# A gated sparsifier over 32 images: the end of the period reordered on TensorE, ScalarE, VectorE and GpSimd

## The reference

```
v = group_norm(x, 32 groups of 16 channels)
r = relu(v)
r = 0 in channels where max(r) - mean(r) < 0.5
bb = 1 - exp(-|max over channels of r - mean over channels of r|)    per pixel
y = bb * r
control1 = sigmoid(mean_pixels(y) @ W1.T)
control3 = relu(mean_pixels(y) @ W3.T), 1.2 where below 1
thres = control1 * control3 * max_pixels(y)                            per channel
out = x + (y where y >= thres, else 0)
```

## Time and profile before

| | |
|---|---|
| median of 3 runs | 1692.47 us (1690.44 to 1693.3) |
| the profiled execution | 1694.59 us, span 1692.8 us |
| VectorE busy | 1459.9 us, 86% |
| ScalarE busy | 1355.9 us, 80% |
| TensorE busy | 1266.6 us, 75% |
| GpSimd busy | 610.5 us, 36% |
| mean granted TensorE clock | 0.868 of full |
| DMA queues | 61.1% and 30.1% of 16 engines' span |

### The profile page before, as it was taken

One profiled execution on the slowest core, in us unless ns is written; L12 is line 12 of the kernel. 1 busy time (PEld: TensorE's weight loads), 2 busy tenths in 40 slices (PEclk: granted clock), 3 DMA queues, 4 the chain that ended last, 5 costly groups with the idle time before them and its releaser, 6 DMA issues.

```text
span 1692.8 us, 26138 instructions
## 1 busy us (share of the span) xinstructions
PE 1266.6 (75%) x9888; PEld 883.0 (52%) x9888; DVE 1459.9 (86%) x2192; ACT 1355.9 (80%) x2177; POOL 610.5 (36%) x446
## 2 busy tenths in 40 slices
PE   3788777887777888777788877778877778877761
PEld 1555455555555555455555555555545555555550
DVE  2588889988889898888998888998888989888896
ACT  6788888788888788888878888888888888888821
POOL 0032334442344442244443243443233444224440
PEclk8988888998788998888898888899888899888885
DMA  9259999999999999999999999999999999999973
GB/s 394 112 127 318 340 355 311 291 314 303 338 350 324 287 316 301 339 343 341 299 303 307 316 343 346 299 309 313 311 342 351 318 299 316 292 340 342 302 228 152
DMA packets 93345, 517.64 MB, mean 306 GB/s; under 512 B 10272, under 2 KB 10272, under 8 KB 93216
## 3 DMA queue, kind: packets, MB, share of 16 engines
q1 hardware_dynamic: 75360, 416.38, 61.1%
q0 software_dynamic: 17856, 99.56, 30.1%
HBM read 310.38 MB, written 205.52 MB: 305 GB/s over the span
## 4 chain that ended last, share of the span: by engine, by line
PE 40%; POOL 28%; ACT 20%; DVE 7%; issue 3%; DMA 1%; DVEq 0%; SPq 0%; ACTq 0%
POOL xs L788 25%; PE ps_gate L331 11%; PE ps_gate L298 10%; PE ps_turn L288 8%; ACT rs L482 6%; ACT rs L457 6%; ACT xs L482 4%; PE ps_gate L318 3%; PE ps_gate L360 2%; PE ps_gate L368 2%; POOL rstd L767 2%; PE ps_gate L306 2%; DVE xs L649 2%; ACT junk L433 1%; DVE max_and_mean L632 1%
## 5 line engine op out<-in xcount | busy, mean ns | idle before, releaser
L632 DVE TENSOR_REDUCE max_and_mean<-ps_turn 128x2 f32<-128x1024 f32 x384 | 463.6, 1218 | 31.8 <-PE ps_turn L288 28.1
L288 PE MATMUL ps_turn<-ident,xs 128*128 128x128 f32 (+1 forms) x1600 | 359.6, 311 | 175.2 <-DVE max_and_mean L632 112.0
L788 POOL TENSOR_TENSOR xs<-xs,rs 128x1568 f32<-128x1568 f32 x124 | 433.3, 3531 | 1.8 <-DVE rs L680 1.8
L779 POOL DMA_DIRECT2D xs<-in_x x124 | 111.5, 968 | 889.4 <-DVE xs L680 796.9
L433 ACT ACTIVATE junk<-xs 128x1568 bf16<-128x1568 f32 x256 | 385.4, 1505 | 9.8 <-ACT junk L433 0.4
L318 PE MATMUL ps_gate<-ident,bb 128*128 128x128 f32 (+1 forms) x1600 | 272.2, 332 | 156.3 <-ACT bb L475 150.8
L288 PE MATMUL ps_turn<-ident,rs 128*128 128x128 f32 (+1 forms) x1600 | 345.7, 302 | 0.0
L318 PEld LDWEIGHTS ps_gate<-ident,bb 128*128 128x128 f32 (+1 forms) x1600 | 248.8, 239 | 175.9 <-DVE ymax_parts L649 163.7
L288 PEld LDWEIGHTS ps_turn<-ident,xs 128*128 128x128 f32 (+1 forms) x1600 | 209.0, 155 | 248.2 <-DVE max_and_mean L632 158.4
L649 DVE CUSTOM_DVE_ANT_0 xs<-xs,ps_gate 128x768 f32<-128x768 f32 (+1 forms) x256 | 243.1, 958 | 48.7 <-PE ps_gate L318 48.5
L457 ACT ACTIVATE xs<-xs,shift,rstd 128x3136 f32<-128x3136 f32 x64 | 192.0, 3001 | 86.0 <-POOL shift L771 80.8
(11 more groups left out here) (80 smaller groups left out, 955.7 us busy)
## 6 DMA issues: line engine op xcount, KB each, us to landing
xs<-in_x SPq DMA_DIRECT2D x260, 784.0 KB, 13.7
out<-xs SPq DMA_DIRECT2D x256, 784.0 KB, 8.2
xs<-in_x POOLq DMA_DIRECT2D x124, 784.0 KB, 10.9
rs<-in_L_conv_W SPq DMA_DIRECT2D x2, 1024.0 KB, 17.5
```

The costliest lines, as they stand in the source:

```text
L288: mm = pe.transpose(ps_turn[0:w, n % 2, b - 2 * i, P * t:P * (t + 1)], r_tile(s, t)[:, P * b:P * b + w], ident[:, :])
L632: ins = dve.tensor_reduce(max_and_mean[:, 2 * i:2 * i + 2, 0], ps_turn[:, n % 2, :, :], AX.X, ALU.max)
L779: pool.dma_start(half(x_tile(s - 1, t), h), dram_half(x_tiles, s - 1, t, h), accum_op=ALU.add).then_inc(x_added[(s - 1) % XR][t][h], 16)
L788: pool.tensor_tensor(o, o, half(r_tile(s - 1, t), h), ALU.add).then_inc(added, 1)
```

## The change

On TensorE all sums of x of the next image come right behind the logits, then the mean rows of the first three tiles in number order, the group statistics, the mean rows of the last tile, a turn, the turning of the means, a turn, and the first spread. ScalarE squares whole tiles (only the first tile stays in halves) into an 8-bit scratch, takes row means and group copy ahead of the copied mean rows, and does the first relu ahead of copying the means; the gate values of group 3 stand ahead of the last relu, three pooling sums ahead of these. VectorE does the first differ behind blocks 3 and 4, the peaks and fails behind all gates of group 2, and the settling right behind the count. GpSimd's affine stands ahead of the fourth accumulating DMA and is one instruction shorter (the row mean comes negated).

```diff
-        junk = sb("junk", [P, HALF], BF16)
+        junk = sb("junk", [P, HW], FP8)
@@ TensorE, per period
-                mean_rows_of(s)
                 if s + 1 < B:
-                    sum_x(s + 1, range(0, 2))
-                turn_means(s)
-                if s + 1 < B:
-                    sum_x(s + 1, range(2, T))
-                turn(s, 3)
-                turn(s, 4)
+                    sum_x(s + 1, range(T))
+                mean_rows_of(s, range(0, T - 1))
                 if s + 1 < B:
                     group_stats(s + 1)
+                mean_rows_of(s, range(T - 1, T))
+                turn(s, 3)
+                turn_means(s)
+                turn(s, 4)
                 spread(s, 0)
@@ TensorE, group statistics
-                pe.wait_ge(squared, 2 * T * (s + 1))
-                for h in range(2):
-                    mm = pe.matmul(ps_group[:, 1, :], group_avg[:, :], squares[:, h, :], start=(h == 0),
-                                   stop=(h == 1), skip_group_check=True)
-                mm.then_inc(group_sums, 1)
+                pe.wait_ge(squared, (T + 1) * (s + 1))
+                first = LOAD_ORDER[0]
+                pe.matmul(ps_group[:, 1, :], group_avg[:, :], squares[:, 0:T], start=True, stop=False,
+                          skip_group_check=True)
+                pe.matmul(ps_group[:, 1, first:first + 1], group_avg[:, :], squares[:, T:T + 1],
+                          start=False, stop=True, skip_group_check=True).then_inc(group_sums, 1)
@@ ScalarE, squares and row means
+            def square_tile(s, n):
                 t = LOAD_ORDER[n]
-                act.wait_ge(x_loaded[s % XR][t][h], 16 * (s // XR + 1))
+                wait_loaded(act, s, t)
+                square(s, t, slice(0, HW), t)
...
-                                          scale=1.0 / (PER_GROUP * HW), accum_out=row_sum[:, :]))
+                                          scale=-1.0 / (PER_GROUP * HW), accum_out=row_sum[:, :],
+                                          saturate=False))
@@ ScalarE, per period
                     square_tile(s + 1, 1)
-                copy_mean_rows(s)
-                if has_next:
                     square_tile(s + 1, 2)
-                copy_means(s)
                 if has_next:
                     square_tile(s + 1, 3)
                     row_means(s + 1)
+                    copy_group(s + 1)
+                copy_mean_rows(s)
+                if has_next:
+                    relu(s + 1, RELU_ORDER[0])
+                copy_means(s)
                 gate_values(s, 0)
-                if has_next:
-                    copy_group(s + 1)
-                    relu(s + 1, RELU_ORDER[0])
                 gate_values(s, 1)
                 if has_next:
                     relu(s + 1, RELU_ORDER[1])
                     relu(s + 1, RELU_ORDER[2])
                 gate_values(s, 2)
-                pool_sum(s, 0, 0)
+                for t in range(3):
+                    pool_sum(s, 0, t)
+                gate_values(s, 3)
                 if has_next:
                     relu(s + 1, RELU_ORDER[3])
-                gate_values(s, 3)
-                for t in range(1, T):
-                    pool_sum(s, 0, t)
+                pool_sum(s, 0, 3)
@@ VectorE, per period
+                if s > 0:
+                    keep_tile(s - 1, KEEP_ORDER[3])
+                block_max(s, 3)
+                block_max(s, 4)
                 differ(s, 0)
-                if s > 0:
-                    keep_tile(s - 1, KEEP_ORDER[3])
-                for i in range(3, 6):
-                    block_max(s, i)
+                block_max(s, 5)
                 differ(s, 1)
...
-                gate(s, 2, 0)
-                gate(s, 2, 1)
-                gate(s, 2, 2)
+                for t in range(T):
+                    gate(s, 2, t)
                 if nxt < B:
                     peaks(nxt)
-                gate(s, 2, 3)
-                if nxt < B:
                     margins(nxt)
                     find_fails(nxt)
                 gate(s, 3, 0)
                 if nxt < B:
                     read_count(nxt)
-                gate(s, 3, 1)
-                if nxt < B:
                     settle_channels(nxt)
-                gate(s, 3, 2)
-                gate(s, 3, 3)
+                for t in range(1, T):
+                    gate(s, 3, t)
@@ GpSimd
-                steps.step(pool.tensor_tensor(mrs[:, :], gst[:, 0, :], rstd[:, :], ALU.mult))
-                steps.wait()
-                pool.tensor_scalar(shift[:, :], mrs[:, :], -1.0, 1.0, ALU.mult, ALU.mult).then_inc(affine_ready, 1)
+                pool.tensor_tensor(shift[:, :], gst[:, 0, :], rstd[:, :], ALU.mult).then_inc(affine_ready, 1)
...
+                    accumulate(s - 1, 0, 0)
+                    accumulate(s - 1, 0, 1)
+                    accumulate(s - 1, 1, 0)
                 if s + 1 < B:
                     affine(s + 1)
+                if s > 0:
+                    accumulate(s - 1, 1, 1)
```

More of the change, by code:

```diff
@@ L6 @@
 F32 = mybir.dt.float32
-BF16 = mybir.dt.bfloat16
+FP8 = mybir.dt.float8e4
 I32 = mybir.dt.int32
@@ L98, in gated_sparsifier @@
         half_neg = sb("half_neg", [P, T])
-        squares = sb("squares", [P, 2, T])
+        squares = sb("squares", [P, T + 1])
         row_sum = sb("row_sum", [P, 1])
@@ L106, in gated_sparsifier @@
         rstd = sb("rstd", [P, T])
-        mrs = sb("mrs", [P, T])
         shift = sb("shift", [P, T])
@@ L290, in turn, with mean_rows_of @@
                 mm.then_inc(t_filled, 1)
-            def mean_rows_of(s):
+            def mean_rows_of(s, tiles):
                 if s > 0:
                     pe.wait_ge(gated, T * (NG * s - 1))
-                for n in range(T * NM):
+                for n in range(NM * tiles.start, NM * tiles.stop):
                     t, j, k = n // NM, n % NM, n % 4
@@ L300, in mean_rows_of @@
                                    stop=(n >= T * NM - 4), skip_group_check=True, tile_position=(0, 32 * k))
-                mm.then_inc(mean_rows_mm, 1)
+                if tiles.stop == T:
+                    mm.then_inc(mean_rows_mm, 1)
             def turn_means(s):
@@ L427, in _, with square, square_half @@
             junk_step = Steps(act, squared)
-            def square_half(s, n, h):
-                t = LOAD_ORDER[n]
-                act.wait_ge(x_loaded[s % XR][t][h], 16 * (s // XR + 1))
[L432 to L438, removed]
+            def square(s, t, cols, part):
+                junk_step.wait()
+                junk_step.step(act.activation(junk[:, cols], x_tile(s, t)[:, cols], ACT.Square,
+                                              scale=float(HW) ** -0.5, accum_out=squares[:, part:part + 1],
+                                              saturate=False))
+            def square_half(s, h):
+                t = LOAD_ORDER[0]
+                act.wait_ge(x_loaded[s % XR][t][h], 16 * (s // XR + 1))
+                square(s, t, slice(HALF * h, HALF * (h + 1)), t if h == 0 else T)
+            def square_tile(s, n):
+                t = LOAD_ORDER[n]
+                wait_loaded(act, s, t)
+                square(s, t, slice(0, HW), t)
             def row_means(s):
@@ L492, in _ @@
             act.wait_ge(consts_ready, 1)
-            for n in range(T):
+            for h in range(2):
+                square_half(0, h)
+            for n in range(1, T):
                 square_tile(0, n)
@@ L503, in _ @@
                 if has_next:
-                    square_half(s + 1, 0, 0)
+                    square_half(s + 1, 0)
                 if s > 0:
@@ L507, in _ @@
                 if has_next:
-                    square_half(s + 1, 0, 1)
+                    square_half(s + 1, 1)
                 if s > 0:
@@ L697, in _ @@
                         keep_tile(s - 1, t)
-                differ(s, 0)
                 if s > 0:
                     keep_tile(s - 1, KEEP_ORDER[3])
-                for i in range(3, 6):
-                    block_max(s, i)
+                block_max(s, 3)
+                block_max(s, 4)
+                differ(s, 0)
+                block_max(s, 5)
                 differ(s, 1)
@@ L768, in affine, with accumulate @@
                 steps.wait()
-                steps.step(pool.tensor_tensor(mrs[:, :], gst[:, 0, :], rstd[:, :], ALU.mult))
-                steps.wait()
-                pool.tensor_scalar(shift[:, :], mrs[:, :], -1.0, 1.0, ALU.mult, ALU.mult).then_inc(affine_ready, 1)
+                pool.tensor_tensor(shift[:, :], gst[:, 0, :], rstd[:, :], ALU.mult).then_inc(affine_ready, 1)
+            def accumulate(s, t, h):
+                pool.wait_ge(kept, T * s + KEEP_ORDER.index(t) + 1)
+                pool.dma_start(half(x_tile(s, t), h), dram_half(x_tiles, s, t, h),
+                               accum_op=ALU.add).then_inc(x_added[s % XR][t][h], 16)
             affine(0)
@@ L775, in _ @@
                 if s > 0:
-                    for t in IN_PLACE:
```

(9 more changed lines are left out.)

## The result

The changed kernel takes 1933.27 us (median of 4 runs, 1929.63 to 1934.3), the kernel before 1692.39 (4 runs, 1690.44 to 1693.3). The ratio is 1.142 with a 95% interval of 1.140 to 1.144: slower by 241 us, 7.8 in each of 31 periods.

A forecast was written before the change was run, and what follows sets the result against it. VectorE with the small chain behind it was taken as the bound. 8.7 - 0.1 = 8.6 us in 30 periods (258), plus 3.5 and 2.5 for first and last, on 1694.59 gave 1958.6, stated as 1955; range 1815 to 1980.

The forecast's parts named there:

- held, clock down: GpSimd's affine held by VectorE's thresholding, spread 0 and turn 5 at half clock: 8.6 us a period, 1955 us; chance 0.55.
- the first rival: GpSimd's affine not held by the thresholding: 1818 us with clock up, 1875 with it down, centre 1835; chance 0.27.
- Affine held to the end of the thresholding: GpSimd's affine, ready at 866.97, waits out VectorE's thresholding of tile 3: full hold of 2.8 us, affine 869.75 to 871.95.
- the relu I had put for them: ScalarE's whole-tile squares priced like a relu of the same size: 3.01 + 0.18 us each.
- The sequel behind the late differ is bare: Gate values, spread and turn 5 no longer hidden under VectorE work; block 5 begins at 878.95, plus 6.8 us.
- my 8.7 us for the start of block 5: VectorE's block 5 begins at 880.85 instead of 872.13: 6.8 us, plus 1.9 for the half clock.
- The clock: TensorE's 5.6 us idle brings half clock to spread and turn 5: 1.4 to 2.3 us more, taken as 1.9.
- held, but the clock stays up: Affine held, TensorE not slowed: net 6.7 us a period, 1902 us; lower end of the forecast's own range, no separate chance.
- End of the period: Last group's gates, peaks, count and settling: gain 1.05 us, bare settling 0.95 us, net minus 0.1 a period.
- a gain of 1.05: VectorE from group 3's differ to its first gate: 5.0 us instead of 6.1, through earlier gate values and less idle.
- the settling follows the copy at once and its 0.95 us are bare: VectorE's settling, today under a 0.94 us gate, lies bare behind the copy of the flag: 0.95 us lost.
- Faster: VectorE loses both waits, logits and last group's gates (140 us), and pays 104: 1658 us; chance 0.05.

The follow-up runs named there:

- x3: Changed kernel with the thresholding of the last tile replaced by a one-operand maximum over it (all images but the last): 1829.9 us, ratio 1.081.
- the probe: Kernel before with a 128x4 memset and a 128x4 product added on GpSimd while VectorE thresholds tile 1: 1690.71 us in one run.
- y1: Kernel before with only the first differ moved behind the last thresholding and blocks 3 and 4 on VectorE: 1828.3 us, ratio 1.081.
- x6: Changed kernel with 22 unused identity products on TensorE between the turn of block 4 and the first spread: 1932.62 us, ratio 1.142.
- x4: Changed kernel with the settling of channels put back behind the second gate of group 3: 1929.23 us, ratio 1.140.
- y3: Kernel before with only the end of the period in the changed kernel's order, the settling left in place: 1650.15 us, ratio 0.975.
- x2: Changed kernel with copying the means and the gate values of group 0 ahead of relu of tile 0 on ScalarE: 1863.55 us, ratio 1.101.

## Why the prediction held, step by step

Forecast 1955, measured 1933. The forecast's own case (held, clock down) is the one that came. The range of 1815 to 1980 would have held the first rival too, so it is the profile and x3, not the time, that tell them apart.

- *Affine held to the end of the thresholding.* Shown by the timeline (989.73 against 989.67), the probe and x3. The first rival, no hold, was priced at 1835; x3, which takes the hold away, came to 1829.9. The group sums were ready 3.2 us ahead of the thresholding's end, 2.8 by the working: the whole-tile squares (2.82 + 0.19 us) were cheaper than the relu I had put for them. Under the hold this was worth nothing. The ground on which I took the full hold was weaker than it looked: the idle of the fourth accumulating DMA ends 0.6 to 1.8 us behind the third thresholding, in the midst of the fourth, while a held computation ends 0.06 us behind the operation that holds it. That the two are the same hold is not shown; that the hold came out as full as this row suggested was in part luck.
- *The sequel behind the late differ is bare.* Shown by y1, 4.4 us a period alone. Of my 8.7 us for the start of block 5, VectorE's waits show 7.9. Measured from the end of the thresholding: differ 5.4 us (5.8 by the working: GpSimd's steps and the relu 0.4 less), spread 0 begins 1.1 behind the differ (0.9), block 5 begins 3.9 behind the spread (4.45); that is the period shown, and the idles before block 5 vary by 0.7 over the inner periods.
- *The clock.* At its place it is 1.7 us a period (x6), 1.9 by the working. As a term of the whole it is not what I took it for: x6 got it back and ended no faster, since the end of the period lost the same. The sum held because the kernel pays for the half clock at one place or another. That the clock would have to stay up at the end of the period too for the rival "held, but the clock stays up", 1902, is what x6 suggests; no run had it up at both.
- *End of the period.* I had a gain of 1.05 and a loss of 0.95. The failed step is "the settling follows the copy at once and its 0.95 us are bare": bare it is (35.8 us over 31 periods, 1.15 each), but x4 shows that covering it is worth 0.1 us a period on balance. And I counted the gain from the missing idle alone, 1.05; by itself (y3) it is 1.35, since the turns and logits came earlier too. In the changed kernel the waits of this part are 0.5 us a period less, against my 0.1. And I added this gain to the loss of the late differ as if the two were independent: y1 shows that the late differ takes the wait of 1.69 away without the new end.
- *Faster,* 1658, by both waits of the end vanishing: not in the changed kernel. But its core, that the gates' wait goes without one as large in its place (10.6 us ahead of the peaks for 48.5), is what y3 shows.

By size, on VectorE: 7.9 - 0.5 + 0.2 (VectorE's 7.5 us more of busy time over 31) = 7.6 us a period against 8.6.

## What to carry to other kernels

Before moving a short instruction behind longer ones on the engine that bounds the kernel, follow who waits for it: here a 0.16 us differ stood at the head of a 5 us chain over three engines, and its early place was worth 4.4 us a period. An operation of GpSimd that reads SBUF gained nothing here from being ready 3.2 us early, since VectorE was in one with two SBUF operands; look for that in the timeline, and keep what is urgent off the tail of such an operation (70 us in x2). Try the parts of a reorder one by one, and on the kernel before: the end of this one is worth 2.5% there, and nothing shows of it in the changed kernel, where the late differ has taken the same wait away.

## What the runs showed of the hardware

- The half clock comes after less idle than I had a row for. Spreads of 12 took 2.90 us behind idles of 5.42, 3.19 (y1), 2.39 (x3) and 2.29 us (x2), against 1.58 in the kernel before. Idle alone doesn't decide it: in the first period of the changed kernel a spread behind 2.29 us took 1.60, and in the kernel before one without idle took 2.46.
- Half clock kept away from one place can come at another: with a filler of 5.08 us the mean clock of the run rose from 0.823 to 0.845, and the time did not change. In the changed kernel periods with the two ends (10.3 and 11.8 us from flag to logits) take turns in no fixed order, and the idle of block 5 moves with them.
- GpSimd's fourth DMA issue, which stands 2.83 us beside two-operand thresholding, takes 0.93 us and doesn't stand once it lies behind the affine. What it waits for there no run isolates, and its idle doesn't end with a thresholding as the held computations do.
